# A transformer block laid out in step tables: feed-forward and projection steps moved forward, the row-maxima DMA moved to ScalarE

## The reference

```python
x = L0_attn_x                                   # (8, 512, 128)
x = x + 0.5 * ffn(layernorm(x), weight, bias, delta_w, delta_act)
x = x + attn(layernorm(x), wq, bq, wk, bk, wv, bv)
x = x + 0.5 * ffn(layernorm(x), weight, bias, delta_w, delta_act)
# ffn:  e = floor(log2(amax of a block)); scale = 2**(e-2) * 2**d; xs = x / scale
#       q = sign(xs) * fp4_round(clip(|xs|, 0, 6)); einsum('bsd,od->bso', scale*q, w_q) + bias
# attn: 16 heads of 8 columns, rotary q and k, softmax(q k^T / sqrt(8)) v
```

## Time and profile before

| | us |
|---|---|
| median of 3 runs | 622.23 |
| lowest, highest | 613.65, 625.24 |
| the profiled execution, its own time | 620.8 |
| its span (first to last instruction) | 618.9 |
| PE busy | 517.9 |
| DVE busy | 452.4 |
| ACT busy | 393.2 |
| POOL busy | 250.7 |

### The profile page before, as it was taken

How to read it: one execution, slowest core, us unless ns; L and a number is a source line. 1 busy time by engine, 2 the same in 40 slices (tenths; PEclk the granted TensorE clock), 3 DMA queues, 4 the chain that set the end, 5 groups by cost and what they waited for, 6 DMA issues and landing times.

```text
span 618.9 us, 10478 instructions
## 1 busy us (share of the span) xinstructions
PE 517.9 (84%) x2724; PEld 177.0 (29%) x2724; DVE 452.4 (73%) x1037; ACT 393.2 (64%) x773; POOL 250.7 (41%) x452
## 2 busy tenths in 40 slices
PE   0453999799979998999889897999889995999862
PEld 0121233233323332333223232333323331322211
DVE  6674879587988797768957598869957784788214
ACT  8343149386958684678837585768747683667750
POOL 6010266215753665345723465346723543011300
PEclk9999999799999998899979899999969996999995
DMA  5016102600161015100350015100440026000000
GB/s 159 1 34 143 27 3 53 153 2 1 35 146 27 20 36 128 45 19 11 92 107 19 6 35 131 44 18 19 96 96 19 2 59 147 13 9 1 6 14 17
DMA packets 21685, 30.84 MB, mean 50 GB/s; under 512 B 4333, under 2 KB 19321, under 8 KB 19321
## 3 DMA queue, kind: packets, MB, share of 16 engines
q1 hardware_dynamic: 21624, 30.13, 20.3%
HBM read 21.34 MB, written 8.39 MB: 48 GB/s over the span
## 4 chain that ended last, share of the span: by engine, by line
PE 54%; DMA 11%; DVE 9%; POOL 8%; issue 7%; ACT 6%; SPq 4%; POOLq 0%; ACTq 0%; DVEq 0%
PE sc L1120 15%; PE ot L1133 14%; PE st L1109 12%; DMA feat_k<-parts_k 8%; PE misc L1074 4%; DMA parts_k<-qkparts_k 3%; SPq L333 3%; DVE negmax L908 2%; ACT probs L639 2%; PE misc L1055 2%; PE misc L1098 2%; POOL rstd_f L404 2%; SPq L335 1%; PE misc L1073 1%; POOL qkparts_k L496 1%
## 5 line engine op out<-in xcount | busy, mean ns | idle before, releaser
L908 DVE TENSOR_REDUCE negmax<-sc 128x1 f32<-128x512 f32 x512 | 331.9, 681 | 106.6 <-PE sc L1120 106.2
L639 ACT ACTIVATE probs<-st 128x512 f32<-128x512 f32 x512 | 273.4, 606 | 127.1 <-PE st L1109 126.4
L1120 PE MATMUL sc<-feat_k,feat_q 96*128 96x512 bf16 x512 | 197.8, 411 | 38.6 <-DMA feat_k<-parts_k 23.9
L1109 PE MATMUL st<-feat_q,feat_k 99*128 99x512 bf16 x512 | 162.1, 395 | 2.9 <-ACT probs L639 2.2
L1133 PE MATMUL ot<-probs,vfeat 128*32 128x512 f32 x1024 | 143.2, 634 | 1.0 <-ACT probs L639 1.0
L1120 PEld LDWEIGHTS sc<-feat_k,feat_q 96*128 96x128 bf16 x512 | 51.2, 100 | 208.7 <-DVE negmax L908 127.4
L1109 PEld LDWEIGHTS st<-feat_q,feat_k 99*128 99x128 bf16 x512 | 50.7, 100 | 71.2 <-ACT probs L639 38.8
L467 POOL TENSOR_TENSOR cosd<-qkv,rope 128x256 f32<-128x256 f32 x28 | 20.4, 728 | 57.6 <-ACT qkv L602 57.5
L404 POOL TENSOR_TENSOR rstd_pj<-ve_pj,nhalf 128x4 f32<-128x4 f32 x8 | 8.3, 1038 | 75.2 <-DVE nm_pj L779 75.2
L446 POOL TENSOR_SCALAR maxparts<-negmax 128x16 bf16<-128x16 f32 x32 | 8.3, 258 | 67.9 <-DVE negmax L908 67.9
L1040 PE MATMUL misc<-identb,xq_f 128*128 128x128 bf16 x64 | 6.9, 236 | 28.9 <-DVE xq_f L842 28.3
(11 more groups left out here) (143 smaller groups left out, 529.0 us busy)
## 6 DMA issues: line engine op xcount, KB each, us to landing
feat_q<-parts_q SPq DMA_DIRECT2D x48, 192.0 KB
feat_k<-parts_k SPq DMA_DIRECT2D x48, 192.0 KB
parts_q<-qkparts_q SPq DMA_DIRECT2D x24, 128.0 KB, 2.3
parts_k<-qkparts_k SPq DMA_DIRECT2D x24, 128.0 KB, 2.3
xres<-in_L_attn_x_dram SPq DMA_DIRECT2D x8, 256.0 KB, 5.1
out_dram<-xres SPq DMA_DIRECT2D x8, 256.0 KB, 2.3
feat_q<-maxrows SPq DMA_DIRECT2D x32, 12.0 KB
wload<-in_L_ffn_weight_dram SPq DMA_DIRECT2D x1, 64.0 KB, 2.4
```

Of the source, the lines that this page charges most:

```text
L639: nc.scalar.activation(probs[:, s % US, j * S:(j + 1) * S], st[:, bank(2 * s + j), :], ACT.Exp, scale=SCALE).then_inc(exp_done, 1)
L908: nc.vector.tensor_reduce(negmax[:, g, j:j + 1], sc[:, bank(16 * g + j), :], AX.X, ALU.max, negate=True).then_inc(sc_maxed, 1)
L1109: nc.tensor.matmul(st[:, bank(2 * s + j), :], feat["k"][par][0:MROWS, h, kb * P:(kb + 1) * P], feat["q"][par][0:MROWS, h, :], start=True, ...
L1120: nc.tensor.matmul(sc[:, bank(16 * g + j), :], feat["q"][par][0:SROWS, h, t * P:(t + 1) * P], feat["k"][par][0:SROWS, h, :], start=True, s ...
```

## The change

The tables FFN1 and PROJ are shifted. FFN1's statistics to quantization stand three steps earlier, its `turn` and `mul` one step. PROJ's early parts stand three steps earlier, its four projections at 25, 27, 29, 30 in place of 27, 30, 31, 35, the transpositions of q and k at 33 and 35 in place of 38 and 39, the parts at 34 to 38 in place of 39 to 42, write and load four steps earlier. FFN2's `turn` and `mul` stand one step later. The DMA of the row maxima is issued by ACT, at 3 mod 8 in place of SP's 2 mod 8. No arithmetic changes.

```diff
-FFN1 = dict(stats=3, rstd=4, norm=6, amax=8, scale=10, expo=11, quant=11, turn=15, mul=16)
-PROJ = dict(stats=20, rstd=21, norm=23, turn=25, qkv=(27, 30, 31, 35), rope=(28, 31, 34, 35), turnqk=(38, 39),
-            rest=(39, 39), mid=(41, 41), low=(42, 42), write=41, load=44, putv=(31, 31, 35, 37))
+FFN1 = dict(stats=0, rstd=1, norm=3, amax=5, scale=7, expo=8, quant=8, turn=14, mul=15)
+PROJ = dict(stats=17, rstd=18, norm=20, turn=22, qkv=(25, 27, 29, 30), rope=(26, 28, 30, 31), turnqk=(33, 35),
+            rest=(34, 36), mid=(35, 37), low=(36, 38), write=37, load=40, putv=(31, 31, 35, 37))
...
-MAX = dict(split=1, turn=2, copy=2, load=2)
+MAX = dict(split=1, turn=2, copy=2, load=3)
...
-            def load_max_rows(b, par, g):
-
-                sp.wait_ge(max_rows, G * b + g + 1)
-                sp.dma_start(feat["q"][par][SROWS:SROWS + PARTS, UH * g:UH * (g + 1), :]
...
+            def load_max_rows(b, par, g):
+
+                act.wait_ge(max_rows, G * b + g + 1)
+                act.dma_start(feat["q"][par][SROWS:SROWS + PARTS, UH * g:UH * (g + 1), :]
...
                         copy_max(nb, g)
+                    for nb, npar, g in turns_of_unit(b, par, s, MAX["load"], 1):
+                        load_max_rows(nb, npar, g)
```

More of the change, by code:

```diff
@@ L65 @@
 MAGIC = 0.5 * 1.5 * 2.0 ** 23
-FFN1 = dict(stats=3, rstd=4, norm=6, amax=8, scale=10, expo=11, quant=11, turn=15, mul=16)
-PROJ = dict(stats=20, rstd=21, norm=23, turn=25, qkv=(27, 30, 31, 35), rope=(28, 31, 34, 35), turnqk=(38, 39),
-            rest=(39, 39), mid=(41, 41), low=(42, 42), write=41, load=44, putv=(31, 31, 35, 37))
-FFN2 = dict(stats=7, rstd=9, norm=11, amax=13, scale=16, expo=16, quant=19, turn=22, mul=23, store=29)
-MAX = dict(split=1, turn=2, copy=2, load=2)
+FFN1 = dict(stats=0, rstd=1, norm=3, amax=5, scale=7, expo=8, quant=8, turn=14, mul=15)
+PROJ = dict(stats=17, rstd=18, norm=20, turn=22, qkv=(25, 27, 29, 30), rope=(26, 28, 30, 31), turnqk=(33, 35),
+            rest=(34, 36), mid=(35, 37), low=(36, 38), write=37, load=40, putv=(31, 31, 35, 37))
+FFN2 = dict(stats=7, rstd=9, norm=11, amax=13, scale=16, expo=16, quant=19, turn=23, mul=24, store=29)
+MAX = dict(split=1, turn=2, copy=2, load=3)
 OUT = dict(copy=2, turn=4, add=6)
@@ L297, in _ @@
                              xv[b]).then_inc(x_loaded[b], 16)
-            def load_max_rows(b, par, g):
-                sp.wait_ge(max_rows, G * b + g + 1)
-                sp.dma_start(feat["q"][par][SROWS:SROWS + PARTS, UH * g:UH * (g + 1), :]
-                             .rearrange("a h (t q) -> a (h t) q", q=P), maxrows[:, g % 2, :]).then_inc(max_loaded[g % 2], 16)
             def write_parts(b, par):
@@ L344, in slot @@
                 for s in range(STEPS):
-                    for nb, npar, g in turns_of_unit(b, par, s, MAX["load"], 1):
-                        load_max_rows(nb, npar, g)
                     for nb, npar in turns_of_batch(b, par, s, PROJ["write"], 2):
@@ L623, in copy_max @@
                 nc.scalar.copy(maxrows[:, g % 2, :], miscb[0:n, 0:P]).then_inc(max_rows, 1)
+            def load_max_rows(b, par, g):
+                act.wait_ge(max_rows, G * b + g + 1)
+                act.dma_start(feat["q"][par][SROWS:SROWS + PARTS, UH * g:UH * (g + 1), :]
+                              .rearrange("a h (t q) -> a (h t) q", q=P), maxrows[:, g % 2, :]).then_inc(max_loaded[g % 2], 16)
             def copy_out(b, g):
```

## The result

The changed kernel takes 657.8 us (median of 4 runs, 656.8 to 661.0) against 622.3 for the kernel before: a ratio of 1.068, with an interval of 1.062 to 1.075, so 6.8% slower. Its profiled execution took 658.7 us, of which the span is 656.8. That is 37.9 us more than the span before; the sum of the prediction was 38.2, its forecast 659 us in a range of 622 to 682.

A forecast was written before the change was run, and what follows sets the result against it. No engine was taken as the bound throughout (PE busy 84%), with DVE setting the pace in steps 7 to 16. Six terms, -34.9 + 31.5 + 16.4 + 12.9 + 3.4 + 8.9 = +38.2, on 620.8 gave 659 us, range 622 to 682.

The forecast's parts named there:

- main case: Whole kernel: slower, the sum of six terms, own range 638 to 675 us; chance 60%.
- The feature wait goes: PE at step 17, batches 1 to 7: waits of 19.3 us and 15.6 us of clock loss vanish, -34.9 us.
- The split behind the rounding: POOL, steps 8 to 10: FFN1's rounding holds the maxima's split; PE waits 5.25 us in six slots, +31.5 us.
- The clock behind these waits: After PE's waits for POOL's split: the clock falls, 2.73 us lost in each of six slots, +16.4 us.
- The wait for ACT: PE at step 4 waits for ACT's copies of k: 2.3 us five times and 1.4 once, +12.9 us.
- DVE's clumps: DVE's work redistributed: +9 in steps 5 to 8, 12.6 back in 11 to 16, +7 in 17 and 18; +3.4 us.
- PE's transposes: Transposes of q and k move to steps 1 and 3, where PE sets the pace, plus prologue: +8.9 us.
- A: Rival: the gain stands alone, the split's waits absent or only replacing other PE waiting; faster, 624 to about 600 us; 13%.
- B: Rival: waits are there but cheap, clock loss absent or harmless and step-4 wait covered; within 2%, 630 us; 19%.
- C: Rival: row-maxima load lands late among feature transfers, step 16's scores wait, or clock falls twice; 665 to 677 or 669; 8%.

The follow-up runs named there:

- ninth experiment: Kernel with FFN1's quant at step 9 and k's transposition at step 37, with the row-maxima load given back to SP at its old step: 654.7 us, ratio 1.055.
- first experiment: Changed kernel with FFN1's quant at step 9 in place of 8: 623.7 us, ratio to the kernel before 1.005.
- filler: Changed kernel with 30 extra multiplications of 384 columns by PE, results unused, where it waited for POOL in slots 0 to 5: 647.5 us.
- fastest kernel: Changed kernel with FFN1's quant at step 9 and k's transposition at step 37: 605.6 us, ratio to the kernel before 0.979.
- the eighth: Changed kernel with FFN1's step table of before and k's transposition two steps later: 618.7 us.
- the third: Changed kernel with both edits, FFN1's quant at step 9 and k's transposition at step 37: 605.6 us, ratio 0.979.
- the seventh: Changed kernel with FFN1's step table of before, the projection staying four steps forward: 607.1 us, ratio 0.978.

## Why the prediction was right

The time was 657.8 where 659 was forecast, by the mechanism of the main case: POOL's held split, PE's wait for it and the clock behind. The direction and most of the size rest on that. That the sum came within 1 us is luck, since errors of 12 us in each direction lie under it.

1. *The feature wait goes, -34.9.* It went, in all seven slots, and batch 0's stayed (3.6 us). The clock behind it was worth more than the 15.6 of the 6 us windows. Slot 1 of the kernel before, where the clock did not fall, gives 31.3 - 1.6 = 29.7 us of work for steps 17 to 32; slots 2 to 5 took 34.7, 38.3, 33.3 and 35.9, of which waits are 8.8, so 14.6 was clock (the granted clock over these stretches, 0.86, 0.91, 0.95 and 0.86, gives 15.0), against the 9.8 that I had counted for them. The term was some 5 us too small. Its side reason, that SP stays free without the row-maxima loads, carried nothing: in the ninth experiment they stand in SP's queue again, and there is still no feature wait but batch 0's, 3.7 us.

2. *The split behind the rounding, +31.5.* Measured 5.11 or 5.12 in each of six slots, 30.7. In slot 1 PE transposes 6.5 us after the last maximum (178.66 against 172.17), where the working had 6.8, and has stood there since 1.4 after it, where it had 1.55. The first experiment takes one number away and the waits with it, and FFN1's table alone brings them into the kernel before.

3. *The clock behind these waits, +16.4.* 16.8 by the windows, 14.7 by the filler in the steps behind.

4. *The wait for ACT, +12.9.* Measured 11.5. The DMA issue, taken at 0.37, costs nothing: in slot 1 it starts at 158.15, beside an exp, and no operation of ACT is late by it. Without it the working gives 1.9 in place of 2.3, where five waits are 1.92 to 2.16. The clock behind them was taken at nothing and cost 5.0. The rows had a warning that the working passed over: behind the wait of 0.97 us, in the earlier trace rows, the clock was 0.50. They held both outcomes, and I rounded them to the cheap one.

   The Trainium skill (TensorE: Matmul & The Clock Gate, What's actually happening) says that the throttled state is the default and activity releases it. I had drawn from it that no single gap's length decides, and up to 10 us. The trace agrees with that much: waits of 2.14 us were followed by 0.72 twice and by 1.00 once.

5. and 6. *DVE's clumps and PE's transposes, +3.4 and +8.9.* Here the terms miss. DVE's added work in steps 5 to 8, taken at 9, shows as 5.0 (35.7 less the 30.7 of waiting). In steps 11 to 16 the recovery came in the size predicted: at full clock they take 11.2 (fastest kernel, slot 1) in place of 13.6, and the clock ate it. Its reason was wrong in part: with the filler, where DVE comes drained, slots 0 to 3 take 10.9, 11.2, 11.4 and 11.4, and in the fastest kernel, where it does not, the same. FFN1's work that left these steps is enough. But steps 17 to 32 take 33.8 or 33.9 us in slots 1 to 5 of the changed kernel, at full clock and with no long wait, 4.1 more than 29.7; the terms had 1.2 there. One of the four projection groups, two rotations and statistics of FFN1 moved in. PE's busy time in these steps of slot 1 went from 29.68 to 31.50, and the rest is short waits. That is 2.9 us x 6 = 17 missed. In return steps 1 to 4 kept their length (7.4 before, 7.2 in the fastest kernel), where the terms added 1.1, since a projection group left them. I moved the transposes of q and k and forgot what else changed place with them. No run takes the projection group by itself, so that it is the cause of the 4.1 us is argued from the tables and PE's busy time.

By the table of steps the prediction reads: 20.6 for steps 1 to 4 (measured 15.0), 40.5 for 5 to 10 (35.7), 3.8 for 11 to 16 (2.1), and -27.9 for 17 to 32 (-15.9). The gain in steps 17 to 32 is 12 us smaller than forecast: 17 for the work that moved in, less the 5 by which term 1 was too small. It is balanced by 12 us that the other steps did not cost. The deciding step, that POOL's order puts the split behind a rounding which waits for DVE, was priced at 31.5 + 16.4 = 47.9 us with its clock and measured 30.7 + 16.8 = 47.5.

One reading was loose: DVE's 15.49 of 16 us was said of steps 7 to 16, but the window, from 164.0 on, begins behind step 9.

*The rivals.* A fell: the waits are there, and without them the time falls by 34.1 us (of it 30.1 in the steps of the wait), so they are not other waits renamed. B fell with the clock at 0.50 to 0.64 in the windows behind and with the uncovered 11.5 us at step 4. C did not happen in the changed kernel, with one wait of 0.9 us, but its mechanism is real. It shows in three kernels without the 5 us wait: 3.0 us in the first experiment, 6.6 in the eighth, 35.7 in the ninth, where SP issues. In the third and the seventh, also without that wait, it is 0.8 and 0.7 us in sum, so the missing wait alone does not bring it out; that the wait for the split gives the feature transfers time to get out of the way is a guess.

The Trainium skill (DMA: Bandwidth & Descriptors, Issuing engines are not separate DMA queues) says that the transfers of all issuing engines interleave on the same 16 engines and that a second issuer only saves issue time. The eighth experiment's trace agrees: a load issued by ACT, with seven feature transfers ahead of it, lets PE go on some 9 us later. In the ninth the issue time is what matters: behind twelve issues of SP's own the small load leaves 8.6 us after the first of them, and with the waits and the clock that is 49 us.

## What to carry over

When a step table moves work forward, look on each in-order engine for what now stands directly behind an operation that waits. Ask what the operation behind it was about to release, since that is paid in full and the clock on top. Then sum the moved work by stretch of steps and not by kind, or what arrives in a stretch besides the step in mind is missed. A part that does nothing alone, as ACT's issue here, may be what makes another part possible, so try it in both kernels before dropping it.

## What the runs showed of the hardware

A DMA issue on ScalarE, 0.74 us on its sequencer, runs beside the exp that is computing: 32 of them changed 619.1 us to 620.1, within the uncertainty.

In the changed kernel, waits of PE of the same length, 2.14 us, left the clock of the next 6 us at 0.72 in slots 3 and 4 and at 1.00 in slot 5; one of 2.16 left 0.72, and those of 1.92 and 1.05 left 1.00. In the kernel with FFN1 alone, waits up to 1.89 left 1.00 and one of 2.57 left 0.72. So a wait of about 2 us has no fixed price: 0 or 1.7 us.

The 512-element clip (`xc`, L853) of FFN1 on VectorE takes 1.34 us at 168.37 in slot 1 of the kernel before, with POOL at work all the while, and 0.42 at 171.15 in the changed kernel, with POOL idle. It is so throughout: the six clips of the kernel before that run beside POOL take 1.06 to 1.37 us, its ten others and all 16 of the changed kernel 0.42 or 0.43. `magic` in that kernel takes 0.43 us also where POOL is at work for 0.35 of it, so not every operation is slowed. No run was made to show the cause.
